# Retention of layer 0: keys placed by VectorE, one batch of look-ahead on TensorE, norm statistics at the end

## The chip, the cores and the metric

One core of a Trainium2 chip runs the whole program. The metric is the device time of one execution in microseconds (us); the kernel before takes 947.5 us in the median of three runs.

## The reference, cut to what matters

The input is 4 batches of 1024 tokens with 128 features, in fp32. After a layer norm, two branches run on it and their sum is added to the input: a retention block (16 heads of 8 features, with its own feed-forward block) and a two-layer local attention network (8 heads of 64, window 64, rotary positions, GELU feed-forward). The change touches the retention:

```python
q = l2_normalize(xn @ qw.T); k = l2_normalize(xn @ kw.T); v = xn @ vw.T
dmask = where(causal, gammas[:, None, None] ** (n - m), 0.0)
sim = einsum('bhnd,bhmd->bhnm', qh, kh) * scale * dmask
yh = einsum('bhnm,bhmd->bhnd', sim, vh)
y = yh.transpose(0, 2, 1, 3).reshape(B, T, D) @ ow.T + ob
```

The kernel computes it block-wise: inside blocks of 32 tokens by masked scores, between blocks and tiles by a carried sum of keys times values per head, with the decay folded into queries and keys.

## The kernel before, in words

Time is cut into 8 tiles of 128 tokens for each of 2 layers of the attention network, 16 steps in all. A step has four slots, one for each batch. `run_bodies` unrolls them, and each engine has its own order written out by hand; every dependency is a semaphore. In a slot, TensorE turns (transposes) the queries and keys of the batch two slots back, computes values for the new batch, scores, turned softmax weights, output turns, the query and key product into pQK, and the weighted values. VectorE takes maxima, subtracts, rotates (`dve_rotate`: cos, then sin, reading pQK), normalises outputs. GpSimd turns the sum of squares into a reciprocal norm (`pool_norm`, L450 and L452), adds the two rotated halves (`pool_add`, L465) and scales (`pool_scale`, L472). ScalarE evacuates PSUM and does exponentials.

In layer 0, the fourth slot of each step also starts the retention of the same tile, and a stretch behind it, called the retention here, finishes it: `pe_retention`, `dve_retention`, `act_retention`, `pool_retention`. For each batch b:

- `pe_retention_project` (L1573): q, k, v of the batch into a PSUM bank (pV or the upper half of pT).
- `act_retention_project` (L731, L736): sums of squares of q and k, then copies of v into avm.
- `pool_retention_norm` (L480, L482): reciprocal norms, ars.
- `dve_retention_qk` (L989): queries and keys times norm and decay, into aqk.
- TensorE turns both (L1587) into pM; ScalarE copies both to aqkT (L755, 128x256).
- `pool_mask_qk` places the keys (kx, L513, which lies in the tensor `hidden`) and the queries (qx, L517, in prT) so that heads of a group don't mix.
- `pe_block_values` (L1607) gives values turned; `act_place_values` (L746) places them in vx. `pe_block_sums` (L1618) gives keys times values per block, which VectorE masks into `before` (L1002).
- `pe_block_scores` (L1654) into pQK, once the rotation of batch 3 has been read out of it; `dve_block_scores` (L1013) applies the causal mask into sm.
- `pe_block_output` (L1628, L1634, L1641) adds the three parts of the output.

TensorE's loop runs k = 0 to 4: turn k, scores k-1, project k+2, placed values and sums k, output k-1. The statistics of the layer norm of the tile before (`pe_ln` L1394 and L1396, `dve_ln` L952 and L955, `pool_ln` L458 and L460) stand in iteration 3. In the next slot VectorE first applies that norm (`dve_ln_apply`, L962) and then adds the retention's residual (`dve_retention_out`, L1021), for which the scores of that slot (`pe_scores`, L1242 and L1255) wait. In the fourth slot VectorE's order is: L989 of retention batch 0, residual of the step before (L912), rotation cos (L842), softmax output (L900, L902), L989 of batch 1, rotation sin, sum of squares (L855). The retention's output is copied by ScalarE at L763 and multiplied at L1660.

Of the kernel before, what the change touches and what calls it, by code (L numbers as in the profile page):

```python
# [12 lines left out]
P = 128  # L13
# [80 lines left out]
def program(nc, a, out):  # L94
    with ExitStack() as ctx:
# [126 lines left out]

        def score_bank(b):

            return pQK[:, 512 * (b % 2):512 * (b % 2) + 512]
# [258 lines left out]
        def pool_retention(eng, t, old):  # L484
            last = NB - 1
            n = count((0, t), last)
            pool_retention_norm(eng, t, 1)
            for b in range(NB):
                pool_mask_qk(eng, t, b)
                if b + 2 < NB:  # L490
                    pool_retention_norm(eng, t, b + 2)
            if old:
                pool_ln(eng, old)
            pool_norm(eng, n, last)
            pool_add(eng, n, last)
            pool_scale(eng, n, last)
            pool_state(eng, t)
# [9 lines left out]
        def pool_mask_qk(eng, t, b):  # L507
# [86 lines left out]
        def act_slot(eng, new, old, ff, k):  # L594
# [30 lines left out]
            if k == NB - 1 and new and new[0] == 0:  # L625
                act_retention_project(eng, new[1], 0)
# [21 lines left out]
            if k == NB - 1 and new and new[0] == 0:  # L648
                act_retention_project(eng, new[1], 1)
# [74 lines left out]
        def act_retention_project(eng, t, b):  # L724
            n = 4 * t + b
            bank = qkv_banks[b % 2]
            eng.wait_ge(A["qkv_mm"], n + 1)
            need(eng, A["rs"], n - 1)
            for g in range(2):
                need(eng, A["sqq"], 2 * n + g)  # L730
                eng.activation(asq[:, :], bank[:, g * P:(g + 1) * P], ACT.Square,  # L731
                               accum_out=ass[:, b % 2, g:g + 1]).then_inc(A["sqq"], 1)
            need(eng, A["kv_mm"], n - 1)
            for c_ in range(NBL):
                rows = slice(0, (c_ + 1) * BL)
                copied = eng.activation(avm[rows, b % 2, c_, :], bank[rows, 2 * P:3 * P], ACT.Copy)  # L736
            copied.then_inc(A["v"], 1)

# [11 lines left out]
        def act_retention(eng, t, old):  # L750
            for k in range(NB):
                n = 4 * t + k
                eng.wait_ge(A["t_mm"], n + 1)
                need(eng, A["qx"], n - 1)
                eng.activation(aqkT[:, k % 2, :, :], pM[:, 0:256].rearrange("p (g n) -> p g n", g=2),  # L755
                               ACT.Copy).then_inc(A["t_ev"], 1)
                if k == 0:
                    act_exp(eng, 1, count((0, t), 1))
                act_place_values(eng, t, k)
                if k + 2 < NB:  # L760
                    act_retention_project(eng, t, k + 2)
# [71 lines left out]
        def dve_rotate(eng, step, k, weighted, ff=None, normed=None):  # L833
# [19 lines left out]
            def sum_squares():  # L853
                need(eng, S["max_ss"], n - 1)
                eng.tensor_reduce(ss[:, k % 2, :], sq[:, :].rearrange("p (h d) -> p h d", d=DH), AX.X,  # L855
                                  ALU.add).then_inc(S["ss_done"], 1)

            if k == NB - 1 and l == 0:
                dve_retention_qk(eng, t, 0)
                if normed:  # L860
                    dve_residual(eng, normed, k)
                eng.wait_ge(S["sq_done"], n + 1)
                turn_cos()
# [3 lines left out]
                turn_sin()  # L867
                sum_squares()
# [4 lines left out]
            sum_squares()  # L873
# [9 lines left out]
            turn_sin()  # L883

# [107 lines left out]

        def dve_retention(eng, t, old):
            eng.wait_ge(LS["qkn_done"], 4 * t + 3)
            for k in range(NB + 1):
                if k > 0:
                    dve_block_scores(eng, t, k - 1)
                if k < NB:
                    n = 4 * t + k
                    eng.wait_ge(A["kv_mm"], n + 1)  # L1000
                    need(eng, A["state"], t)
                    eng.tensor_tensor(before[:, k, :, :], pS[:, 0:P].rearrange("p (c n) -> p c n", c=NBL),  # L1002
                                      same_head, ALU.mult).then_inc(A["kvm"], 1)
                if k + 2 < NB:
                    dve_retention_qk(eng, t, k + 2)
                if k == NB - 1 and old:
                    dve_ln(eng, old)
# [295 lines left out]
        def pe_slot(eng, new, old, ff, k):  # L1303
# [271 lines left out]

        def pe_retention(eng, t, old):

            eng.wait_ge(LS["pt_ev"], 4 * t + 1)
            if old:
                eng.wait_ge(LS["xr_done"], count(old, NB - 1) + 1)  # L1580
            for k in range(NB + 1):
                if k < NB:
                    n = 4 * t + k
                    eng.wait_ge(A["qk"], 2 * n + 2)
                    need(eng, A["t_ev"], n)
                    for g in range(2):
                        mm = eng.transpose(pM[:, g * P:(g + 1) * P], aqk[:, k % 2, g, :], ident)  # L1587
                    mm.then_inc(A["t_mm"], 1)
                if k > 0:
                    pe_block_scores(eng, t, k - 1)  # L1590
                if k + 2 < NB:
                    pe_retention_project(eng, t, k + 2)
                if k == NB - 1 and old:
                    eng.wait_ge(A["t_ev"], 4 * t + 4)
                    pe_ln(eng, old)
                if k < NB:
                    pe_block_values(eng, t, k)
                    pe_block_sums(eng, t, k)
                if k > 0:
                    pe_block_output(eng, t, k - 1)  # L1600
# [142 lines left out]
```

## Time and profile before

| what | value |
|---|---|
| runs | 947.5, 945.47, 947.5 us; median 947.5 |
| profiled execution | 948.3 us, span of its trace 946.5 us |
| mean granted clock of TensorE | 0.989 of full |
| TensorE, matmuls | 863.4 us busy, 91% of the span |
| VectorE | 634.5 us, 67% |
| ScalarE | 559.2 us, 59% |
| GpSimd | 631.5 us, 67% |

Rows of a timeline give start, length, engine, line, operation, output and inputs, count, and in brackets the idle time before with what ended it. PE is TensorE's matmuls, PEld its weight loads, DVE VectorE, ACT ScalarE, POOL GpSimd. Matmuls are pipelined: the starts of the weight loads show how fast a group of them issues. A group's length on PE includes the latency of its last one. Tile 3 is the fourth of eight in layer 0; its retention output is copied at 274.77 us.

### The profile page before, as it was taken

The page shows a single profiled execution, that of the slowest core. Times are in us where ns is not written, and L with a number is a line of the kernel's source. Part 1 is how long each engine was busy: PE and PEld are TensorE (multiplying, and loading weights), DVE is VectorE, ACT ScalarE, POOL GpSimd, SP SyncE. Part 2 cuts the span into 40 slices and gives each one's busy share as a digit, 9 for nine tenths or more (in the row PEclk, how much of TensorE's full clock was granted, in tenths as well). Part 3 has the DMA queues.
Part 4 walks back from the last instruction along what each step waited for, and adds up shares of the span by engine and source line. Part 5 has one row for each costly group of instructions (what it writes and reads, how often), then busy time and mean ns, then how long its engine had stood idle before and what let it go on. Part 6 is the DMA issues. An engine that isn't in the chain of part 4 may idle for free.

```text
span 946.5 us, 26551 instructions
## 1 busy us (share of the span) xinstructions
PE 863.4 (91%) x10918; PEld 587.4 (62%) x10918; DVE 634.5 (67%) x1087; ACT 559.2 (59%) x1109; POOL 631.5 (67%) x503
## 2 busy tenths in 40 slices
PE   0678899989989899899998989999999999999998
PEld 0346666666666667666576565757575757575756
DVE  5875575766757666667576776767676767676754
ACT  0335575666756657567566555666666666666663
POOL 4588586676775876758667666676767676767641
PEclk9979999999999999999999999999999999999999
DMA  9211120211201112021021111212121212121201
GB/s 297 52 26 23 35 46 17 46 23 26 55 17 38 30 22 53 11 40 41 16 46 22 32 43 26 54 26 65 37 65 37 65 37 67 37 66 35 57 1 35
DMA packets 127890, 41.82 MB, mean 44 GB/s; under 512 B 103794, under 2 KB 127004, under 8 KB 127644
## 3 DMA queue, kind: packets, MB, share of 16 engines
q1 hardware_dynamic: 122516, 38.82, 18.3%
q10 hardware_dynamic: 5256, 1.31, 0.8%
q8 instruction: 88, 1.44, 0.6%
q14 instruction: 30, 0.25, 0.1%
HBM read 9.70 MB, written 2.10 MB: 12 GB/s over the span
## 4 chain that ended last, share of the span: by engine, by line
PE 62%; DVE 15%; POOL 10%; ACT 6%; issue 5%; DMA 1%; DVEq 0%; SPq 0%; POOLq 0%; ACTq 0%
PE pQK L1352 9%; PE pT L1266 5%; PE pT L1223 5%; PE pV L1321 5%; PE pS L1255 5%; PE pS L1282 4%; DVE m L842 4%; PE pM L1434 4%; PE pM L1300 4%; POOL rn L452 3%; PE pQK L1654 3%; PE pT L1412 3%; DVE ss L855 2%; POOL m L465 2%; PE pS L1242 2%
## 5 line engine op out<-in xcount | busy, mean ns | idle before, releaser
L452 POOL TENSOR_TENSOR rn<-rn,half_neg 128x16 f32<-128x16 f32 x64 | 187.5, 2929 | 5.3
L465 POOL TENSOR_TENSOR m<-m 128x1024 f32<-128x1024 f32 x64 | 150.7, 2355 | 0.0
L450 POOL TENSOR_SCALAR rn<-ss 128x16 f32<-128x16 f32 x64 | 16.3, 254 | 187.7 <-DVE ss L855 186.4
L1352 PE MATMUL pQK<-wqkv,hT 128*128 128x512 f32 x256 | 125.0, 611 | 5.2 <-DVE m L842 5.2
L472 POOL TENSOR_TENSOR qkn<-m,rn 128x1024 f32<-128x1024 f32 x64 | 121.7, 1902 | 5.0
L890 DVE TENSOR_REDUCE mx<-pS 128x8 f32<-128x1024 f32 x64 | 78.0, 1219 | 60.8 <-PE pS L1255 60.7
L672 ACT ACTIVATE prT<-pT 128x1024 f32<-128x1024 f32 x64 | 65.5, 1024 | 68.8 <-PE pT L1266 68.6
L635 ACT ACTIVATE sq<-pQK 128x1024 f32<-128x1024 f32 x64 | 65.4, 1022 | 35.4 <-PE pQK L1352 35.2
L855 DVE TENSOR_REDUCE ss<-sq 128x16 f32<-128x1024 f32 x64 | 77.6, 1212 | 7.1 <-ACT sq L635 6.9
L666 ACT ACTIVATE kT<-pT 128x512 f32<-128x512 f32 x64 | 38.2, 597 | 72.8 <-PE pT L1223 72.8
L892 DVE TENSOR_TENSOR pr<-pS,mx 128x1024 f32<-128x1024 f32 x64 | 78.4, 1225 | 2.2
L707 ACT ACTIVATE pr<-pr 128x1024 f32<-128x1024 f32 x64 | 67.3, 1051 | 18.8 <-DVE pr L892 18.6
L842 DVE TENSOR_TENSOR m<-pQK,rope 128x1024 f32<-128x1024 f32 x64 | 76.3, 1215 | 0.0
L842 DVE TENSOR_TENSOR m<-pQK,tab 128x1024 f32<-128x1024 f32 x64 | 76.2, 1212 | 0.0
L1282 PEld LDWEIGHTS pS<-vmix,prT 128*64 128x64 f32 x1024 | 64.5, 137 | 18.5 <-issue 13.1
L1223 PE MATMUL pT<-cst,qkn 128*128 128x128 f32 x512 | 70.4, 282 | 5.6 <-POOL qkn L472 4.9
L1321 PE MATMUL pV<-wqkv,hT 128*128 128x512 f32 x128 | 69.7, 628 | 5.7 <-DVE gst L1121 2.7
L1282 PE MATMUL pS<-vown,prT 128*64 128x65 f32 x1024 | 73.3, 225 | 0.0
L1282 PE MATMUL pS<-vmix,prT 128*64 128x65 f32 x1024 | 73.3, 225 | 0.0
L1352 PEld LDWEIGHTS pQK<-wqkv,hT 128*128 128x128 f32 x256 | 45.4, 195 | 42.8 <-issue 32.7
L1266 PE MATMUL pT<-cst,pr 128*128 128x128 f32 x512 | 70.0, 280 | 0.0
L1255 PE MATMUL pS<-kT,qT 64*64 64x128 f32 x2048 | 68.5, 273 | 0.0
(224 smaller groups left out, 1878.2 us busy)
## 6 DMA issues: line engine op xcount, KB each, us to landing
vmix<-vown SPq DMA_DIRECT2D x124, 128.0 KB, 2.7
kT<-kT SPq DMA_DIRECT2D x60, 128.0 KB, 2.6
x<-in_L_attn_x SPq DMA_DIRECT2D x4, 512.0 KB, 8.9
hT<-xnT SPq DMA_DIRECT2D x64, 32.0 KB, 1.9
xs<-in_L_attn_x SPq DMA_DIRECT2D x8, 256.0 KB, 3.1
hT<-x2T SPq DMA_DIRECT2D x64, 32.0 KB, 1.9
out<-aqkT SPq DMA_DIRECT2D x7, 256.0 KB, 2.2
wqkv<-in_L_ffn_wqkv SPq DMA_DIRECT2D x2, 768.0 KB, 9.6
```

Source lines behind the costliest of these rows:

```text
L452: eng.tensor_tensor(rn[:, k % 2, :], rn[:, k % 2, :], half_neg[:, 0:2 * H], ALU.pow).then_inc(S["rn_done"], 1)
L465: eng.tensor_tensor(m1[:, k % 2, :], m1[:, k % 2, :], m2[:, :], ALU.add).then_inc(S["add_done"], 1)
L472: eng.tensor_tensor(qkn[:, k % 2, :].rearrange("p (h d) -> p h d", d=DH), m1[:, k % 2, :].rearrange("p (h d) -> p h d", d=DH), rn[:, k % 2 ...
L842: eng.tensor_tensor(m.rearrange(shape, g=2, h=H, **sizes), src, by, ALU.mult).then_inc(S["mul_done"], 1)
L855: eng.tensor_reduce(ss[:, k % 2, :], sq[:, :].rearrange("p (h d) -> p h d", d=DH), AX.X, ALU.add).then_inc(S["ss_done"], 1)
L892: eng.tensor_tensor(pr[:, b % 2, :, :], sc, mx[:, :].unsqueeze(2).broadcast_to([P, H, P]), ALU.subtract).then_inc(S["sub_done"], 1)
L1223: mm = eng.transpose(pT[:, j * P:(j + 1) * P], qkn[:, b % 2, j * P:(j + 1) * P], ident)
L1255: mm = eng.matmul(pS[64 * w:64 * w + 64, col0:col0 + P], qT[r, j, 64 * w:64 * w + 64], keys, start=False, stop=True, skip_group_check=True)
L1266: mm = eng.transpose(pT[:, j * P:(j + 1) * P], pr[:, b % 2, j, :], ident)
L1282: mm = eng.matmul(pS[64 * w:64 * w + 64, col0:col0 + DH + 1], prT[:, i, 64 * w:64 * w + 64], (vown if w else vmix)[b][:, 2 * j + g, :], st ...
L1321: eng.matmul(pV[:, :], hT[:, k, :], wqkv[:, l, 1024:1536], start=True, stop=True).then_inc(S["v_mm"], 1)
L1352: mm = eng.matmul(pQK[:, g * 512:(g + 1) * 512], hT[:, k, :], wqkv[:, l, g * 512:(g + 1) * 512], start=True, stop=True)
```

## The change

- The keys are placed by VectorE (`dve_place_keys`) straight from the turned PSUM bank, with the same shape as before on GpSimd; ScalarE copies only the turned queries (128x128), and GpSimd places only queries. For batch 0, this placement waits for the weighted values of the slot, since qx shares its memory with the softmax weights.
- Turn 0 moves into the fourth slot, ahead of the weighted values, and writes to pT; turns 1 to 3 use pM.
- TensorE runs placed values and block sums of batch b+1 ahead of the output of batch b, and turns b+1 behind scores b.
- The layer-norm statistics move behind scores 3 on TensorE, and behind the last causal mask on VectorE.
- GpSimd scales batch 2 after the retention norm of batch 0. The orders on ScalarE and VectorE are written out; the sum of squares of batch 3 and the exponential of batch 1 stand near their ends.

```diff
+def turned_bank(b):
+    return pM if b else pT
...
     retain = k == NB - 1 and new and new[0] == 0
+    if k == 2 and new and new[0] == 0:
+        pool_norm(eng, count(new, k), k)
+        pool_add(eng, count(new, k), k)
+        return
     if retain:

         pool_retention_norm(eng, new[1], 0)
+        pool_scale(eng, count(new, 2), 2)
         return
     if old and k == NB - 1:
         pool_ln(eng, old)
...
     last = NB - 1
     n = count((0, t), last)
+    pool_place_queries(eng, t, 0)
     pool_retention_norm(eng, t, 1)
-    for b in range(NB):
-        pool_mask_qk(eng, t, b)
-        if b + 2 < NB:
-            pool_retention_norm(eng, t, b + 2)
+    pool_retention_norm(eng, t, 2)
+    pool_place_queries(eng, t, 1)
+    pool_retention_norm(eng, t, 3)
+    pool_place_queries(eng, t, 2)
+    pool_place_queries(eng, t, 3)
     if old:
...
+def pool_place_queries(eng, t, b):
     n = 4 * t + b
     shape = [P, NBL, NG, BL]
     eng.wait_ge(A["t_ev"], n + 1)
-    need(eng, A["st_mm"], n - 1)
-    eng.tensor_tensor(kx[:, b % 2, :, :, :],
-                      aqkT[:, b % 2, 1, :].rearrange("p (c n) -> p c n", c=NBL).unsqueeze(2).broadcast_to(shape),
-                      place_mask.unsqueeze(1).unsqueeze(3).broadcast_to(shape), ALU.mult).then_inc(A["kx"], 1)
+    if b == 0:
+        eng.wait_ge(LS["o_mm"], count((0, t), 0) + 1)
     need(eng, A["y_mm"], n - 1)
     eng.tensor_tensor(qx[:, b % 2, :, :, :],
                       aqkT[:, b % 2, 0, :].rearrange("p (c n) -> p c n", c=NBL).unsqueeze(2).broadcast_to(shape),
...
+
+def act_retention_queries(eng, t, b):
+    n = 4 * t + b
+    eng.wait_ge(A["t_mm"], n + 1)
+    need(eng, A["qx"], n - 1)
+    eng.activation(aqkT[:, b % 2, 0, :], turned_bank(b)[:, 0:P], ACT.Copy).then_inc(A["t_ev"], 1)
 def act_place_values(eng, t, b):
...
     placed.then_inc(A["vx"], 1)

 def act_retention(eng, t, old):
...
+    act_retention_queries(eng, t, 0)
+    act_retention_values(eng, t, 1)
+    act_retention_squares(eng, t, 2)
+    act_place_values(eng, t, 0)
+    act_retention_values(eng, t, 2)
+    act_retention_queries(eng, t, 1)
+    act_place_values(eng, t, 1)
+    act_retention_squares(eng, t, 3)
+    act_retention_queries(eng, t, 2)
+    act_retention_values(eng, t, 3)
+    act_place_values(eng, t, 2)
+    act_retention_queries(eng, t, 3)
+    act_exp(eng, 1, count((0, t), 1))
+    act_place_values(eng, t, 3)
     eng.wait_ge(A["y_mm"], 4 * t + 4)
     eng.activation(ayT, pY, ACT.Copy).then_inc(A["yt"], 1)

...
     if k == NB - 1 and l == 0:
         dve_retention_qk(eng, t, 0)
+        eng.wait_ge(S["sq_done"], n + 1)
+        turn_cos()
         if normed:
             dve_residual(eng, normed, k)
-        eng.wait_ge(S["sq_done"], n + 1)
-        turn_cos()
+        dve_place_keys(eng, t, 0)
+        turn_sin()
         if weighted:
             dve_output(eng, weighted[2])
         dve_retention_qk(eng, t, 1)
-        turn_sin()
-        sum_squares()
         return
...
+def dve_place_keys(eng, t, b):
+    n = 4 * t + b
+    shape = [P, NBL, NG, BL]
+    eng.wait_ge(A["t_ev"], n + 1)
+    need(eng, A["st_mm"], n - 1)
+    eng.tensor_tensor(kx[:, b % 2, :, :, :],
+                      turned_bank(b)[:, P:2 * P].rearrange("p (c n) -> p c n", c=NBL).unsqueeze(2).broadcast_to(shape),
+                      place_mask.unsqueeze(1).unsqueeze(3).broadcast_to(shape), ALU.mult).then_inc(A["kx"], 1)
+def dve_block_sums(eng, t, b):
+    eng.wait_ge(A["kv_mm"], 4 * t + b + 1)
+    need(eng, A["state"], t)
+    eng.tensor_tensor(before[:, b, :, :], pS[:, 0:P].rearrange("p (c n) -> p c n", c=NBL),
+                      same_head, ALU.mult).then_inc(A["kvm"], 1)
 def dve_retention(eng, t, old):
+    dve_block_sums(eng, t, 0)
     eng.wait_ge(LS["qkn_done"], 4 * t + 3)
...
+    dve_block_scores(eng, t, 0)
+    dve_place_keys(eng, t, 1)
+    dve_retention_qk(eng, t, 2)
+    dve_block_sums(eng, t, 1)
+    dve_block_scores(eng, t, 1)
+    dve_place_keys(eng, t, 2)
+    dve_retention_qk(eng, t, 3)
+    dve_block_sums(eng, t, 2)
+    dve_block_scores(eng, t, 2)
+    dve_place_keys(eng, t, 3)
+    dve_block_sums(eng, t, 3)
+    dve_sum_squares(eng, count((0, t), NB - 1), NB - 1)
+    dve_block_scores(eng, t, 3)
+    if old:
+        dve_ln(eng, old)
 def dve_block_scores(eng, t, b):
     n = 4 * t + b
...
+    if k == NB - 1 and new and new[0] == 0:
+        pe_retention_turn(eng, new[1], 0)
...
+def pe_retention_turn(eng, t, b):
+    n = 4 * t + b
+    eng.wait_ge(A["qk"], 2 * n + 2)
+    need(eng, A["kx"], n)
+    for g in range(2):
+        mm = eng.transpose(turned_bank(b)[:, g * P:(g + 1) * P], aqk[:, b % 2, g, :], ident)
+    mm.then_inc(A["t_mm"], 1)
 def pe_retention(eng, t, old):
...
     if old:
         eng.wait_ge(LS["xr_done"], count(old, NB - 1) + 1)
...
+    pe_retention_project(eng, t, 2)
+    eng.wait_ge(A["kx"], 4 * t + 1)
+    pe_block_values(eng, t, 0)
+    pe_block_scores(eng, t, 0)
+    pe_block_sums(eng, t, 0)
+    pe_retention_turn(eng, t, 1)
+    pe_block_values(eng, t, 1)
+    pe_retention_project(eng, t, 3)
+    pe_block_sums(eng, t, 1)
+    pe_block_output(eng, t, 0)
+    pe_block_scores(eng, t, 1)
+    pe_retention_turn(eng, t, 2)
+    pe_block_values(eng, t, 2)
+    pe_block_sums(eng, t, 2)
+    pe_block_output(eng, t, 1)
+    pe_block_scores(eng, t, 2)
+    pe_retention_turn(eng, t, 3)
+    pe_block_values(eng, t, 3)
+    pe_block_sums(eng, t, 3)
+    pe_block_output(eng, t, 2)
+    pe_block_scores(eng, t, 3)
+    if old:
+        eng.wait_ge(A["kx"], 4 * t + 4)
+        pe_ln(eng, old)
+    pe_block_output(eng, t, 3)
 def pe_block_values(eng, t, b):
```

## Rows read from the trace of the kernel before

**Rows 1.** The page: engine shares

```profile
PE 863.4 (91%) x10918; PEld 587.4 (62%) x10918; DVE 634.5 (67%) x1087; ACT 559.2 (59%) x1109; POOL 631.5 (67%) x503
```

**Rows 2.** Busy time by engine in one retention stretch

```profile
core 0: us, PE busy (x) PEld busy (x) DVE busy (x) ACT busy (x) POOL busy (x), PEclk, DMA share, GB/s
...
253.70:274.77 21.07, 17.85 (x514) 14.06 (x513) 11.78 (x32) 12.52 (x55) 15.48 (x21) 1.00 0.09 18
```

**Rows 3.** Timeline of tile 3, front edge of the retention

```profile
254.13 1.90 POOL L472 TENSOR_TENSOR qkn<-m,rn 128x1024 f32<-128x1024 f32 x1
...
254.13 0.19 ACT L731 ACTIVATION_READ_ACCUMULATOR asq<-pV 128x1 f32 x1
...
255.40 1.05 PE L1300 MATMUL pM<-oT,wo 128*128 128x128 f32 x8
...
257.05 0.61 DVE L989 SCALAR_TENSOR_TENSOR aqk<-pV,ars,cst 128x128 f32<-128x128 f32 x2 [3.19 <-POOL ars L482]
...
257.31 0.22 PE L1282 MATMUL pS<-vmix,prT 128*64 128x65 f32 x1
...
259.14 0.69 DVE L902 TENSOR_TENSOR o<-pS,rec 128x512 f32<-128x512 f32 x1
...
260.26 1.22 DVE L842 TENSOR_TENSOR m<-pQK,rope 128x1024 f32<-128x1024 f32 x1
...
261.39 1.21 DVE L855 TENSOR_REDUCE ss<-sq 128x16 f32<-128x1024 f32 x1
```

**Rows 4.** Timeline of tile 3: TensorE in the loop

```profile
262.53 0.81 PE L1573 MATMUL pT<-aT,xa 128*128 128x384 f32 x2
...
264.60 0.20 PEld L1587 LDWEIGHTS pM<-cst,aqk 128*128 128x128 f32 x2
...
268.57 0.20 PEld L1587 LDWEIGHTS pM<-cst,aqk 128*128 128x128 f32 x2
...
268.88 0.97 PEld L1654 LDWEIGHTS pQK<-prT,hidden 128*128 128x128 f32 x8
...
269.77 0.47 PEld L1394 LDWEIGHTS pM<-cst,xr 128*128 128x128 f32 x4
...
270.79 0.35 PEld L1607 LDWEIGHTS pT<-aT,xa 128*32 128x32 f32 x32
...
271.04 0.21 PEld L1618 LDWEIGHTS pS<-avm,aqk 128*32 128x32 f32 x8
...
271.18 0.28 PEld L1628 LDWEIGHTS pS<-prT,state 128*32 128x32 f32 x8
...
272.13 0.97 PEld L1654 LDWEIGHTS pQK<-prT,hidden 128*128 128x128 f32 x8
```

**Rows 5.** Timeline of tile 3: ScalarE, GpSimd and VectorE in the loop

```profile
266.50 1.10 ACT L746 ACTIVATE vx<-pT 32x128 f32<-32x128 f32 x4
...
267.77 1.04 POOL L517 TENSOR_TENSOR prT<-aqkT,cst 128x512 f32<-128x512 f32 x1
...
270.08 0.69 DVE L1013 TENSOR_TENSOR m<-pQK,cst 128x512 f32<-128x512 f32 x1 [1.84 <-PE pQK L1654]
```

**Rows 6.** Timeline of tile 3: the tail and the next slot

```profile
271.76 0.88 DVE L952 BATCH_NORM_STATS2 lbst<-pM 128x6 f32<-128x128 f32 x4
...
274.53 1.37 DVE L962 TENSOR_SCALAR hn<-pM,lmv,lrs 128x128 f32<-128x128 f32 x4 [0.51 <-POOL lrs L460]
...
274.77 0.60 ACT L763 ACTIVATE gg<-pS 128x512 f32<-128x512 f32 x1 [2.33 <-PE pS L1641]
...
276.64 0.75 DVE L1021 SCALAR_TENSOR_TENSOR x<-pS,col,xnT 128x512 f32<-128x512 f32 x1 [0.75 <-PE pS L1660]
...
286.81 0.26 POOL L450 TENSOR_SCALAR rn<-ss 128x16 f32<-128x16 f32 x1 [3.63 <-DVE ss L855]
```

**Rows 7.** Timeline of tile 0, front edge and retention output

```profile
76.21 0.61 DVE L989 SCALAR_TENSOR_TENSOR aqk<-pV,ars,cst 128x128 f32<-128x128 f32 x2 [1.33 <-POOL ars L482]
...
94.66 0.60 ACT L763 ACTIVATE gg<-pS 128x512 f32<-128x512 f32 x1 [3.33 <-PE pS L1641]
```

More of the change, by code:

```diff
@@ L505, in pool_state @@
             eng.tensor_tensor(state[:, :, :], state[:, :, :], before[:, :, NBL - 1, :], ALU.add).then_inc(A["state"], 1)
-        def pool_mask_qk(eng, t, b):
+        def pool_place_queries(eng, t, b):
             n = 4 * t + b
@@ L625, in act_slot @@
             if k == NB - 1 and new and new[0] == 0:
-                act_retention_project(eng, new[1], 0)
+                act_retention_squares(eng, new[1], 0)
+                act_retention_values(eng, new[1], 0)
             if k == 0 and turned:
@@ L648, in act_slot @@
             if k == NB - 1 and new and new[0] == 0:
-                act_retention_project(eng, new[1], 1)
+                act_retention_squares(eng, new[1], 1)
             else:
@@ L722, in act_gelu, with act_retention_squares @@
                            bias=b1e[0:m, l, 1, k:k + 1]).then_inc(S["gelu_done"], 1)
-        def act_retention_project(eng, t, b):
+        def act_retention_squares(eng, t, b):
             n = 4 * t + b
-            bank = qkv_banks[b % 2]
             eng.wait_ge(A["qkv_mm"], n + 1)
@@ L730, in act_retention_project, with act_retention_values @@
                 need(eng, A["sqq"], 2 * n + g)
-                eng.activation(asq[:, :], bank[:, g * P:(g + 1) * P], ACT.Square,
+                eng.activation(asq[:, :], qkv_banks[b % 2][:, g * P:(g + 1) * P], ACT.Square,
                                accum_out=ass[:, b % 2, g:g + 1]).then_inc(A["sqq"], 1)
-            need(eng, A["kv_mm"], n - 1)
+        def act_retention_values(eng, t, b):
+            need(eng, A["kv_mm"], 4 * t + b - 1)
             for c_ in range(NBL):
                 rows = slice(0, (c_ + 1) * BL)
-                copied = eng.activation(avm[rows, b % 2, c_, :], bank[rows, 2 * P:3 * P], ACT.Copy)
+                copied = eng.activation(avm[rows, b % 2, c_, :], qkv_banks[b % 2][rows, 2 * P:3 * P], ACT.Copy)
             copied.then_inc(A["v"], 1)
+        def act_retention_queries(eng, t, b):
[3 more added lines that the diff above has]
+            eng.activation(aqkT[:, b % 2, 0, :], turned_bank(b)[:, 0:P], ACT.Copy).then_inc(A["t_ev"], 1)
         def act_place_values(eng, t, b):
@@ L750, in act_retention @@
         def act_retention(eng, t, old):
[L751 to L761, printed above, removed]
+            act_retention_queries(eng, t, 0)
[12 more added lines that the diff above has]
+            act_place_values(eng, t, 3)
             eng.wait_ge(A["y_mm"], 4 * t + 4)
@@ L851, in turn_sin @@
                 turn(m2[:, :], rot, sin, "p (g h s d) -> p g h s d", s=2, d=32)
[L853 to L856, printed above, removed]
             if k == NB - 1 and l == 0:
                 dve_retention_qk(eng, t, 0)
+                eng.wait_ge(S["sq_done"], n + 1)
+                turn_cos()
                 if normed:
                     dve_residual(eng, normed, k)
-                eng.wait_ge(S["sq_done"], n + 1)
-                turn_cos()
+                dve_place_keys(eng, t, 0)
+                turn_sin()
                 if weighted:
@@ L872, in dve_rotate @@
             eng.wait_ge(S["sq_done"], n + 1)
-            sum_squares()
+            dve_sum_squares(eng, n, k)
             if weighted:
@@ L883, in dve_rotate, with dve_sum_squares @@
             turn_sin()
+        def dve_sum_squares(eng, n, k):
+            need(eng, LS["max_ss"], n - 1)
+            eng.tensor_reduce(ss[:, k % 2, :], sq[:, :].rearrange("p (h d) -> p h d", d=DH), AX.X,
+                              ALU.add).then_inc(LS["ss_done"], 1)
         def dve_scores(eng, b, n):
@@ L991, in dve_retention_qk @@
                                          op1=ALU.mult).then_inc(A["qk"], 1)
+        def dve_place_keys(eng, t, b):
[11 more added lines that the diff above has]
+                              same_head, ALU.mult).then_inc(A["kvm"], 1)
         def dve_retention(eng, t, old):
+            dve_block_sums(eng, t, 0)
             eng.wait_ge(LS["qkn_done"], 4 * t + 3)
[L995 to L1007, printed above, removed]
+            dve_block_scores(eng, t, 0)
[13 more added lines that the diff above has]
+                dve_ln(eng, old)
         def dve_block_scores(eng, t, b):
@@ L1574, in pe_retention_project @@
                        stop=True).then_inc(A["qkv_mm"], 1)
+        def pe_retention_turn(eng, t, b):
[5 more added lines that the diff above has]
+            mm.then_inc(A["t_mm"], 1)
         def pe_retention(eng, t, old):
-            eng.wait_ge(LS["pt_ev"], 4 * t + 1)
             if old:
                 eng.wait_ge(LS["xr_done"], count(old, NB - 1) + 1)
[L1581 to L1600, printed above, removed]
```

## The prediction

> **What bounds the kernel now.** I read the page's engine shares first: TensorE is busy 91% of the span [rows 1]. That is an average over stages, so I cut out the stage that the change touches, the retention of layer 0, eight times one tile, and asked for the busy time in one such stretch [rows 2]: in 21.07 us TensorE is busy 17.85, VectorE 11.78, ScalarE 12.52, GpSimd 15.48. No engine is full. Then I read the timeline of tile 3 in that stretch, front edge, middle and tail. All layouts below are for tile 3, in us from the span's start.
>
> Front edge: GpSimd starts the 1.90 us scale of batch 2 at 254.13, though the squares of retention batch 0 are ready at 254.13 + 0.19 = 254.32; VectorE's normalised queries and keys (L989) begin only at 257.05 after 3.19 idle [rows 3]. Middle: the weight loads of TensorE give the spacing of its groups when nothing holds them [rows 4]. One batch costs 0.31 (turn) + 0.89 (scores) + 0.25 (placed values) + 0.14 (block sums) + 0.95 (output) = 2.54 us, where before takes about 4 us (turn of batch 2 at 264.60, of batch 3 at 268.57). The causal mask L1013 of batch 2 follows 1.84 us of idle VectorE [rows 5]: the loop is turn, ScalarE copy, two GpSimd placements of 1.04 one behind the other, scores, mask, output. Tail: norm statistics L952 at 271.76, norm applied at 274.53, block residual x at 276.64, for which the next slot's scores wait; the retention output is copied at 274.77 [rows 6].
>
> **The change, part by part.**
>
> *GpSimd.* Four key placements (1.04 each, like the query placement [rows 5]) leave each tile. The scale of batch 2 goes behind the norm of retention batch 0. That norm took from about 256.0 to 257.0 (from the end of the scale to the start of L989), so 1.0. New: 254.4 to 255.4, scale to 257.3. Who needs the scale: the mask of batch 0 and the next slot's turn, both after 260.
>
> *VectorE.* L989 of batch 0: 255.5 to 256.1, 1.6 earlier. Rotation cos (1.22, and 1.13 from start to start [rows 3]) to 257.2, residual to 257.4. Added: key placement of batch 0. No row shows it; it reads PSUM, 128x512, with a broadcast. Below it the mask L1013 of the same shape, 0.69 [rows 5]; above it the 128x1024 rotation, 1.22 [rows 3]. Taken 0.69, same size and same source. 257.3 to 258.0. Rotation sin to 259.1 (before 260.26 + 1.22 = 261.5), output of batch 0 to 260.0 (before 259.14 + 0.69 = 259.8).
>
> *TensorE, front.* Output projection ends at 255.40 + 1.05 = 256.45 [rows 3]. New and ahead of the values: the turn of batch 0, issued 256.3 to 256.6, result 256.8. It waits for L989, done 256.1: no wait. Values, 0.93 (before, from about 256.4 to the last one at 257.31 [rows 3]), issued to 257.5, results at 257.85. Projection of batch 2, 0.84 with its issue gap (0.81 matmul [rows 4]), to 258.4; placed values 0 to 258.6. Scores 0 wait for rotation sin: 259.2 instead of 261.5. Sums 0 at 260.1.
>
> *New waits on GpSimd.* The placement of queries 0 now waits for the last value matmul, and the norm of batch 1 is queued behind it: 257.9 to 258.9, norm to 260.0. VectorE's L989 of batch 1 waits for it to 260.0 and ends at 260.65, 0.3 later than before. Turn 1 on TensorE 260.7. So TensorE idles here 0.55 + 0.5.
>
> *The loop.* Turn 1, placed values 1, projection 3, sums 1: 260.7 + 0.31 + 0.25 + 0.84 + 0.14 = 262.2. Output 0 to 263.2, scores 1 to 264.1, turn 2 to 264.4, placed values and sums to 264.8, output 1 to 265.7 (mask 1: scores end 264.35, 0.69, so 265.1, in time). Scores 2 need queries 2: turn result 264.55, ScalarE copy 0.25, GpSimd 1.04, so 266.0; to 266.9. Turn 3 to 267.2, values and sums 267.6, output 2 to 268.55; queries 3 give scores 3 at 268.8, to 269.7. (The 128x128 ScalarE copy: between 0.19 and the 0.60 of a 128x512 one [rows 3, 6]; taken 0.25, four times smaller data; at 0.6 it adds 0.35 in two places.) Period 3.1 to 3.3, against 4.
>
> *Hidden moves.* ScalarE is busy 12.52 of 21.07 [rows 2], 1.10 a batch for placed values [rows 5]; placed values 3 end near 269.8 and are used at 271.2. The exponential of batch 1 moves to about 267.7 to 268.7; its reader is a turn in the next slot, after 275. The sum of squares of batch 3 (1.21 [rows 3]) runs on VectorE at 268.6 to 269.8 while scores 3 are computed; mask 3 could not start before 270.0. GpSimd's norm of batch 3 stands behind the layer norm, both 0.9 earlier than before; GpSimd idles 3.63 before its next norm [rows 6], so this has cover. SP: the value copy that follows the values comes 0.35 later; its reader is a slot away.
>
> *Norm statistics.* Their transposes move from before placed values 3 to behind scores 3: 269.77 to 270.79 before, 1.02 [rows 4]; now 269.7 to 270.7, result 270.85. So the batch loop gains 3.3 us at scores 3 (272.13 before [rows 4]) and the norm's place gives all of it back to the norm. Statistics to norm applied is 274.53 - 271.76 = 2.77; now 270.9 + 2.77 = 273.65, 0.9 earlier. Norm applied 1.37, so the block residual can start at 275.0. By the other branch output 3 goes to 271.7, copied at 271.85 (2.9 earlier), and from the copy to the block residual is 276.64 - 274.77 = 1.87, so 273.7. VectorE's order puts the norm first: 275.0 decides, against 276.64. **Gain 1.6 per tile**; 1.3 of the 2.9 are lost to the new wait, which takes the place of 0.75 idle.
>
> Tile 0 has no norm of a tile before. Its squares are ready late anyway, L989 of batch 0 stands at 76.21 [rows 7]. By the same steps turn 1 falls at 81.2, and from turn 1 to the copy is 271.85 - 260.7 - 1.0 (no norm) = 10.2. Copy at about 91.5 to 92, against 94.66: gain 3.0.
>
> **Sum.** 948.3 (the profiled run, 946.5 span and 1.8 around it) - 7 x 1.6 - 3.0 = 934.1. The median of runs, 947.5, lies 0.8 below the profiled run; I leave that in the range. Forecast 934.
>
> *A rule against it.* TensorE's record is busy for 17.85 of 21.07 us [rows 2], and the change removes none of its work; GpSimd and ScalarE are less busy. The Trainium skill, Perfetto Trace Analysis, Identifying the Most-Contended Engine, has one optimise the engine with the highest occupancy, which here would promise nothing from moving vector work; the same section warns that matmul busy time misleads. The loads, busy 14.06 of 21.07 [rows 2], agree with the warning.
>
> *A second.* VectorE's rotation and sum start 1.13 apart though the first lasts 1.22 [rows 3]. The Trainium skill, VectorE: DVE Perf Modes, The DRAIN you can't avoid, says that an operation starts only when the pipe is empty, with exceptions; by full lengths the front would be some 0.4 longer and the sum 3 us higher. This trace shows the overlap, so the rows stand.
>
> **The rivals.**
> *Front edge not released.* If TensorE's new turn or GpSimd's new wait comes out later (key placement at 1.22, or the norm of batch 0 held up by work in between), up to 1.6 goes. With 1.22: 0.53 a batch, less the slack of 0.1 at L989, of 0.3 at scores 2 and 3, makes about 0.9 at the norm: gain 0.7 x 7 + 2 = 7, so 941. For it: TensorE, GpSimd and VectorE each wait on each other at 260. Against: nothing shown on VectorE with this shape costs over 0.69. Times 938 to 944.
> *Norm hidden.* If the layer norm didn't decide, 7 x 2.9 + 3 = 23, so 925. Against: the order on VectorE.
> *No change,* as the busy share of TensorE taken as its limit has it: each batch at the recorded lengths (about 3.5 us) leaves nothing: 948. Against: the spacings [rows 4].
> *Slower: the norm too late.* Everything from the norm's transposes to the next scores is a fixed 5.3 us after scores 3. It decides when these end after 269.7 + 1.6 = 271.3. Should the loop keep its 4 us, because VectorE now carries placement, mask, sums and L989 and is a step in both its halves, scores 3 end at 272.13 + 0.89 = 273.0: 1.7 per tile lost, 948.3 + 12 = 960. For it: keys, mask and sums in one queue, three waits per batch. Against: that is 0.69 + 0.69 + 0.61 [rows 3, 5] and the small mask of the sums, some 2.3 of 3.2.
>
> **How the numbers follow.** Norm decides, 0.52 (930 to 938). Front not released, 0.22. Norm hidden, 0.08. No change, 0.07. Slower, 0.11. A difference of 0.3%, 2.8 us, is about what a measurement of this kernel tells. Faster 0.82, same 0.07, slower 0.11. Range 925 to 943: from the norm hidden to the top of the second case; left out is 0.18.
>
> **What would show it.** VectorE's L989 near 255.5 relative to the same slot, key placement 0.69, turns 3 to 3.3 us apart; the retention output copied 2.9 earlier but the block residual only 1.6 earlier, VectorE going straight from the applied norm to it, and TensorE idle about 2 before the next slot's first scores; stretches after this unchanged in length. Wrong if the placement takes over 0.9, if turns stay 4 apart, or if GpSimd's norm of batch 1 comes after 261.

## The result, and the profile after

The changed kernel takes 936.48 us in the median of four runs (932.63 to 938.07), the kernel before 946.49 beside it (944.82 to 947.5): ratio 0.989, 95% interval 0.9855 to 0.9925, some 10 us faster. The prediction was 934 with a range of 925 to 943. Its profiled execution took 936.44, span 934.6, against 948.3 and 946.5.

The page of the changed kernel, engine shares and the shares of the chain that ended last:

```profile
PE 862.5 (92%) x10918; PEld 587.3 (63%) x10918; DVE 654.5 (70%) x1119; ACT 555.6 (59%) x1109; POOL 599.9 (64%) x471
...
PE 68%; DVE 14%; ACT 6%; issue 5%; POOL 4%; DMA 1%; DVEq 0%; SPq 0%; POOLq 0%; ACTq 0%
```

TensorE does the work of before (863.4 us) in a shorter span; 32 instructions moved from GpSimd to VectorE. The same stretch of tile 3 as [rows 2], from the same point to the copy of the retention output, busy time by engine (columns as there):

```profile
248.63:267.80 19.17, 18.04 (x514) 14.13 (x513) 14.15 (x35) 12.18 (x55) 10.05 (x14) 1.00 0.10 19
```

It lasts 19.17 instead of 21.07, and TensorE's busy time hardly moves (18.04 after 17.85): what went is its waiting. Against [rows 3] all times of tile 3 stand 5.07 earlier at the start of the stretch (the last read of a square sum at 249.06 against 254.13). Timeline of the front edge:

```profile
249.06 0.19 ACT L740 ACTIVATION_READ_ACCUMULATOR asq<-pV 128x1 f32 x1
...
249.64 0.71 POOL L491 TENSOR_TENSOR ars<-ars,half_neg 128x2 f32<-128x2 f32 x1
...
250.33 1.90 POOL L481 TENSOR_TENSOR qkn<-m,rn 128x1024 f32<-128x1024 f32 x1
...
250.39 0.61 DVE L1011 SCALAR_TENSOR_TENSOR aqk<-pV,ars,cst 128x128 f32<-128x128 f32 x2 [1.60 <-POOL ars L491]
...
252.28 0.68 DVE L1021 TENSOR_TENSOR hidden<-pT,cst 128x512 f32<-128x512 f32 x1
...
252.88 1.21 DVE L863 TENSOR_TENSOR m<-pQK,rope 128x1024 f32<-128x1024 f32 x1
...
254.89 0.61 DVE L1011 SCALAR_TENSOR_TENSOR aqk<-pT,ars,cst 128x128 f32<-128x128 f32 x2
```

Queries and keys of batch 0 wait 1.60 instead of 3.19 for their norm, as laid out; the new placement of keys is L1021, 0.68. Timeline of TensorE in the loop, weight loads and one matmul:

```profile
255.59 0.20 PEld L1626 LDWEIGHTS pM<-cst,aqk 128*128 128x128 f32 x2 [0.20 <-DVE aqk L1011]
...
259.14 0.25 PEld L1626 LDWEIGHTS pM<-cst,aqk 128*128 128x128 f32 x2
...
262.02 0.25 PEld L1626 LDWEIGHTS pM<-cst,aqk 128*128 128x128 f32 x2
...
263.44 0.22 PE L1664 MATMUL pT<-aT,xa 128*32 128x32 f32 x1 [0.55 <-issue]
...
265.41 0.47 PEld L1438 LDWEIGHTS pM<-cst,xr 128*128 128x128 f32 x4
```

The turns are 3.55 and 2.88 apart (laid out 3.4 and 2.8), where before has 3.97 for the second of these distances [rows 4]. In the middle of the placed values of batch 3, TensorE then stops for 0.55 with nothing to wait for that the profile shows. The tail, against [rows 6]:

```profile
266.55 0.89 DVE L974 BATCH_NORM_STATS2 lbst<-pM 128x6 f32<-128x128 f32 x4
...
267.80 0.60 ACT L784 ACTIVATE gg<-pS 128x512 f32<-128x512 f32 x1 [2.96 <-PE pS L1698]
...
270.62 0.74 DVE L1063 SCALAR_TENSOR_TENSOR x<-pS,col,xnT 128x512 f32<-128x512 f32 x1
...
271.50 0.41 PE L1284 MATMUL pS<-mask 64*64 64x512 bf16 x4 [1.02 <-DVE x L1063]
```

The residual row has no idle time ahead of it any more (0.75 before): VectorE comes straight from the applied norm, and TensorE waits 1.02 for the residual. From the copy to the residual it is 270.62 - 267.80 = 2.82, against 1.87 before. In the tiles whose copy no stop has delayed it is 3.1 to 3.2. This distance is the best single reading of the case, and the table below has it for every kernel.

### The profile page after: what moved, and what is told of

Same layout as the page of the kernel before. It is cut to its first block, busy times and chain, and to the rows that moved or that the text cites. A ratio compares the mean times of both kernels' runs of the same rounds, so it can differ in the third digit from the quotient of the medians.

```text
span 934.6 us, 26589 instructions
## 1 busy us (share of the span) xinstructions
PE 862.5 (92%) x10918; PEld 587.3 (63%) x10918; DVE 654.5 (70%) x1119; ACT 555.6 (59%) x1109; POOL 599.9 (64%) x471
## 4 chain that ended last, share of the span: by engine, by line
PE 68%; DVE 14%; ACT 6%; issue 5%; POOL 4%; DMA 1%; DVEq 0%; SPq 0%; POOLq 0%; ACTq 0%
PE pQK L1394 9%; PE pT L1308 6%; PE pS L1324 5%; PE pS L1297 5%; PE pT L1265 5%; PE pV L1363 5%; PE pM L1478 4%; PE pQK L1711 4%; DVE m L863 4%; PE pM L1342 4%; PE pT L1456 3%; PE pS L1284 2%; DVE hn L984 2%; PE pM L1336 2%; POOL lrs L469 2%
## 5 line engine op out<-in xcount | busy, mean ns | idle before, releaser
L622 ACT ACTIVATE vown<-pV 128x512 f32<-128x512 f32 x64 | 38.2, 597 | 52.7 <-DMA vmix<-vown 29.6
```

## How the stage is measured in the experiments

Differences of a few us between single executions are not all made in the retention. The block residual of tile 0 stood anywhere from 92.97 to 96.52 us in the profiles of this study, whatever the kernel, and the change of layers, between the last residual and the first output DMA, took 125.5 to 131.9 us. So beside the times I read, from each timeline, the mean of the six distances between block residuals from tile 1 to tile 7, the shortest of them (a tile without stalls), and the distance from copy to residual in that tile. Where two tiles share the shortest distance, the last column is that of tile 7. The stage numbers come from one profiled execution of each kernel, whose time can lie some us off the median (short_norm: 930.1 against 933.6).

| kernel | median us | ratio to before, interval | mean per tile | shortest | copy to residual |
|---|---|---|---|---|---|
| before | 946.5 | | 61.28 | 60.99 | 1.86 |
| x1_first_before | 948.0 | 1.0009 (0.9994 to 1.0025) | 61.30 | 60.99 | 1.86 |
| short_norm_before | 951.2 | 1.0052 (1.0032 to 1.0072) | 61.41 | 60.98 | 1.86 |
| scale_only | 940.5 | 0.9937 (0.9914 to 0.9959) | 60.48 | 60.13 | 1.86 |
| the change | 936.5 | 0.989 (0.9855 to 0.9925) | 59.95 | 59.60 | 3.1 |
| scale_back | 947.9 | 1.0005 (0.9991 to 1.0018) | 61.52 | 61.15 | 3.2 |
| keys_twice | 944.2 | 0.9977 (0.9965 to 0.999) | 60.76 | 60.70 | 3.2 |
| keys_on_pool | 958.9 | 1.0131 (1.0108 to 1.0154) | 62.78 | 62.77 | 3.2 |
| norm_early | 933.2 | 0.985 (0.9819 to 0.9881) | 59.37 | 58.79 | 1.86 |
| short_norm | 933.6 | 0.987 (0.985 to 0.989) | 58.92 | 58.49 | 2.1 |
| x1_first | 928.3 | 0.9806 (0.9785 to 0.9826) | 58.85 | 58.50 | 1.87 |
| x1_norm_early | 932.9 | 0.9851 (0.9819 to 0.9884) | 59.30 | 58.78 | 1.86 |

## Does the norm decide in the changed kernel?

Six kernels on one question. First, VectorE's order in the next slot turned round; the residual's four BATCH_NORM_STATS move into `dve_retention_stats`.

```diff
+if old and k == 0 and old[0] == 0:
+    dve_retention_out(eng, old[1])
 if ff and k == 0 and not is_scaled_early(ff):
     dve_ln_apply(eng, ff)
-if old and k == 0 and old[0] == 0:
-    dve_retention_out(eng, old[1])
...
 if turned:
     dve_scores(eng, turned[1], turned[2])
+if old and k == 0 and old[0] == 0:
+    dve_retention_stats(eng, old[1])
```

> The changed kernel with VectorE's order in the next slot turned round: the block residual first, then the layer norm applied, and the residual's statistics behind the score maxima. Theory N (in the changed kernel the norm decides when the block residual starts): by the changed kernel's trace the residual stands 3.1 to 3.2 us after the copy of the retention output in most tiles, and 1.87 after it in the kernel before where only the output decided; the waits go down by 0.5 to 1.35 per tile, 8.1 over tiles 1 to 7, so 936.5 - 8 = 928.5 us. Rival T (TensorE or the path through the retention output decides, the norm's wait is covered): no change, 935.5 to 937.5. Rival D (the norm applied becomes late for its own turn on TensorE, a new wait): 0 to 3 us gained.

Measured 928.31 (926.42 to 929.75), theory N's number. Its timeline in tile 3:

```profile
265.78 0.60 ACT L784 ACTIVATE gg<-pS 128x512 f32<-128x512 f32 x1 [2.36 <-PE pS L1702]
...
267.65 0.75 DVE L1065 SCALAR_TENSOR_TENSOR x<-pS,col,xnT 128x512 f32<-128x512 f32 x1 [1.65 <-PE pS L1721]
...
268.32 1.36 DVE L986 TENSOR_SCALAR hn<-pM,lmv,lrs 128x128 f32<-128x128 f32 x4
```

VectorE again waits for the output's product before the residual, 1.87 after the copy, and the norm is applied behind it. The norm is not on the path any more, and its own turn has cover. This version beats both kernels, in an interval that doesn't touch that of the change. Its gain of 8.2 us matches the sum of the waits that the trace of the change shows over tiles 1 to 7 (copy to residual, less 1.86 each: 8.15). Rival D, a new wait at the norm's own turn, did not come.

The same edit on the kernel before:

> The kernel before with VectorE's order in the next slot turned round as in x1_first. Theory N: there the residual waited for the output's product in every tile with the norm done 0.65 to 1.56 earlier, so nothing is gained: 946.5 within 1.5 us. Rival (the order is worth its 8 us whatever the rest): 938.5.

Measured 948.04, ratio 1.0009, per tile 61.30 against 61.28: nothing. The order is worth something only where the norm comes late, which the change brought about.

The norm made shorter instead, in both kernels. The edit is in `pool_ln`:

```diff
+if step[0] == 0:
+    eng.tensor_scalar(lrs[:, :], lmv[:, :, 1], EPS, None, ALU.add).then_inc(S["ln_rs"], 1)
+    return
 eng.tensor_scalar(lvar[:, :], lmv[:, :, 1], EPS, None, ALU.add).then_inc(S["ln_eps"], 1)
-eng.wait_ge(S["ln_eps"], ct + 1)
+eng.wait_ge(S["ln_eps"], ct + 1 - NT)
```

> The changed kernel with the reciprocal root of layer 0's layer norm left out on GpSimd (variance plus epsilon is used as the factor, which changes the result of the feed-forward of layer 0): 1.04 us and its wait fewer between statistics and norm applied, 1.1 per tile. Theory N: up to 1.1 in each of seven tiles, in the ones with less slack less, 7 us: 929.5. Rival T: no change, 936.5.

> The same root left out of the kernel before. Theory N says that there the norm did not decide, since VectorE idled 0.65 to 1.56 before the block residual: no change, 946.5 within 1.5. A rival under which the root is on the path in both kernels: 939.5.

Both kernels leave the root out, so only their times are of use. By these both miss: 933.57 instead of 929.5, and 951.23 instead of 946.5. By the stage both hit. Per tile the changed kernel gains 59.95 - 58.92 = 1.03, and the distance from copy to residual falls from 3.1 to 2.1; the kernel before has 61.41 against 61.28 and 1.86 as ever. What hides it stands elsewhere: from the last block residual to the first output DMA short_norm_before takes 131.93 us where before takes 127.17, and short_norm 129.23 against the change's 127.01. The timeline of short_norm_before there shows two operations on 4 values each:

```profile
573.79 2.27 DVE L1134 TENSOR_TENSOR gtmp<-gst,gsc 128x4 f32<-128x4 f32 x1
576.10 1.99 DVE L1135 TENSOR_SCALAR gsh<-gtmp,col 128x4 f32<-128x4 f32 x1
```

In the kernel before the same two take 0.16 and 0.23, so 3.9 of the 4.8 us are these two. In short_norm they take 2.27 and 1.99 as well, but its change of layers is only 2.2 longer; the other 1.9 of its miss stay open. The last section shows what the two operations wait for.

Last, the norm moved forward in the retention, in the changed kernel and in x1_first.

```diff
+if old:
+    eng.wait_ge(A["kx"], 4 * t + 4)
+    pe_ln(eng, old)
 pe_block_scores(eng, t, 3)
-if old:
-    eng.wait_ge(A["kx"], 4 * t + 4)
-    pe_ln(eng, old)
...
 dve_block_sums(eng, t, 3)
-dve_sum_squares(eng, count((0, t), NB - 1), NB - 1)
-dve_block_scores(eng, t, 3)
 if old:
     dve_ln(eng, old)
+dve_block_scores(eng, t, 3)
+dve_sum_squares(eng, count((0, t), NB - 1), NB - 1)
```

> The changed kernel with the norm's transposes ahead of the scores of batch 3 on TensorE and its statistics ahead of the last causal mask on VectorE (the sum of squares goes last). The norm comes about 1 us earlier, the retention output about 0.7 later than in the changed kernel. Theory N: the block residual 0.6 earlier in seven tiles, 4 us, so 932.5. Rival T (the retention output decides): 0.7 later in seven tiles, 941.5.

> x1_first and norm_early together. With the block residual ahead of the applied norm, theory N says that the path through the retention output decides, and norm_early puts the norm's transposes and statistics on that path: the copy of the output came about 0.7 us later in an undisturbed tile there, so 0.5 to 0.7 later in seven tiles than x1_first, 928.3 + 4 = 932.5, the opposite sign of what norm_early did to the changed kernel alone (936.5 to 933.2). Rival (an early norm is good in itself, for GpSimd or for the next slot): at or below 928.

Measured 933.17 and 932.94: the same move gains 0.58 per tile on the changed kernel (59.95 to 59.37) and loses 0.45 on x1_first (58.85 to 59.30). In the shortest distances, where stops of TensorE play no part, it gains 0.81 and loses 0.28, and from L989 to the copy norm_early is 0.45 longer in tile 7 (17.03 against 16.58), not the 0.7 that was expected. By the intervals alone neither difference is certain, since each pair just overlaps; the signs in the stage and both medians are as theory N has them. In norm_early the residual is back to waiting for the output (copy, norm applied, residual of its tile 3):

```profile
268.86 0.60 ACT L784 ACTIVATE gg<-pS 128x512 f32<-128x512 f32 x1 [3.42 <-PE pS L1698]
268.93 1.36 DVE L984 TENSOR_SCALAR hn<-pM,lmv,lrs 128x128 f32<-128x128 f32 x4
...
270.72 0.75 DVE L1063 SCALAR_TENSOR_TENSOR x<-pS,col,xnT 128x512 f32<-128x512 f32 x1 [0.43 <-PE pS L1717]
```

Rival T fell in x1_first, short_norm and norm_early. In x1_first and x1_norm_early the path through the retention output is the one that decides, as theory N has it once the norm is out of the way.

## What holds the front edge and the loop?

The order of GpSimd alone, put into the kernel before (scale_only); scale_back takes the same lines out of the changed kernel:

```diff
+if k == 2 and new and new[0] == 0:
+    pool_norm(eng, count(new, k), k)
+    pool_add(eng, count(new, k), k)
+    return
 if retain:
     pool_retention_norm(eng, new[1], 0)
+    pool_scale(eng, count(new, 2), 2)
     return
```

> The kernel before with one edit: GpSimd does the scale of batch 2 behind the retention norm of batch 0. Theory F (the front edge is held by that scale, whatever the rest): VectorE's queries and keys of batch 0 come 1.6 us earlier, the rotation sin about 1.1 earlier, since the residual now waits for the output projection, so the scores of batch 0 come 1.0 earlier and, as the loop stays as it is, the block residual too: 1.0 in seven tiles, 7 us, so 939.5. Rival L (the gain comes from the look-ahead and the keys on VectorE): within 1 us of 946.5.

> The changed kernel with the scale of batch 2 put back in its slot, ahead of the retention norm. Theory F: VectorE's queries and keys of batch 0 come 1.6 later, and with them the turn of batch 0, the weighted values behind it, the output of batch 0 and the keys of batch 1: 1.5 later in seven tiles, 10.5 us, so 947, no faster than before. Rival L: the loop makes up for it, at most 3 us slower than the changed kernel, 939.5.

Measured 940.49 and 947.94, so rival L fell in both. One instruction's place brings 6 of the 10 us by itself, and without it the rest of the change brings nothing (ratio 1.0005). The first row of scale_back shows VectorE's wait as long as in [rows 3], 3.20, the second TensorE's wait for the turn of batch 0:

```profile
256.64 0.61 DVE L1011 SCALAR_TENSOR_TENSOR aqk<-pV,ars,cst 128x128 f32<-128x128 f32 x2 [3.20 <-POOL ars L491]
...
257.31 0.44 PE L1626 MATMUL pT<-cst,aqk 128*128 128x128 f32 x2 [1.27 <-DVE aqk L1011]
```

It costs more there (1.55 in the shortest tile) than it gives on the kernel before (0.86). The change put the turn of batch 0 ahead of the weighted values, and TensorE stands still for 1.27 in front of it: whatever makes queries and keys of batch 0 late now also holds these, the output of the slot and the keys behind them.

The keys back on GpSimd: the four calls of `dve_place_keys` go, and

```diff
 def pool_place_queries(eng, t, b):
...
+    need(eng, A["st_mm"], n - 1)
+    eng.tensor_tensor(kx[:, b % 2, :, :, :],
+                      aqkT[:, b % 2, 1, :].rearrange("p (c n) -> p c n", c=NBL).unsqueeze(2).broadcast_to(shape),
+                      place_mask.unsqueeze(1).unsqueeze(3).broadcast_to(shape), ALU.mult).then_inc(A["kx"], 1)
     if b == 0:
         eng.wait_ge(LS["o_mm"], count((0, t), 0) + 1)
...
-    eng.activation(aqkT[:, b % 2, 0, :], turned_bank(b)[:, 0:P], ACT.Copy).then_inc(A["t_ev"], 1)
+    eng.activation(aqkT[:, b % 2, :, :], turned_bank(b)[:, 0:2 * P].rearrange("p (g n) -> p g n", g=2),
+                   ACT.Copy).then_inc(A["t_ev"], 1)
```

And the keys placed twice on VectorE, in `dve_place_keys`:

```diff
+    spare = hn[:, :, :].rearrange("p c (g n) -> p c g n", g=NG)
+    for place in (spare, kx[:, b % 2, :, :, :]):
+        placed = eng.tensor_tensor(place,
...
+    placed.then_inc(A["kx"], 1)
```

> The changed kernel with the keys placed by GpSimd, ahead of the queries of the same batch, and ScalarE copying both, as before. If two placements of 1.04 in a row belong to the loop (theory P): 0.3 to 0.4 later at the front and 1.1 at scores 2 and at scores 3, 2.6 to 2.8 per tile in eight tiles, 22 us, so 955 to 959, slower than the kernel before. Rival O (the order alone brings the gain, TensorE being the limit in the loop): 936 to 940.

> The changed kernel with each placement of keys on VectorE done twice, once into a spare tile: 0.60 more per batch. By the layout of the prediction: 0.55 later at queries and keys of batch 1, 0.3 more at scores 2 and at scores 3, so 1.15 per tile in eight tiles, 9 us: 945.7. If VectorE is the bound of the loop (rival V), all four count in full: 2.4 per tile, 19 us: 955.5. If it has cover everywhere: 936.5.

keys_on_pool measured 958.86, slower than the kernel before by 1.3%, 3.2 per tile more than the change in the shortest tile (2.6 to 2.8 expected). Two placements stand one behind the other again, and the look-ahead has no slack for them. TensorE stands still for 1.30 before the scores; the profile names no releaser, but the queries that they need are placed until 263.96 + 1.04 = 265.00, and the scores before that start at 265.10:

```profile
262.96 1.04 POOL L524 TENSOR_TENSOR hidden<-aqkT,cst 128x512 f32<-128x512 f32 x1 [0.92 <-ACT aqkT L759]
...
263.96 1.04 POOL L530 TENSOR_TENSOR prT<-aqkT,cst 128x512 f32<-128x512 f32 x1
...
266.27 0.69 DVE L1056 TENSOR_TENSOR m<-pQK,cst 128x512 f32<-128x512 f32 x1 [2.13 <-PE pQK L1712]
...
269.09 1.13 PE L1712 MATMUL pQK<-prT,hidden 128*128 128x128 f32 x8 [1.30 <-issue]
```

The turns are 4.21 and 3.98 apart, as in the kernel before (4.20 and 3.98), while the norm comes at the end of the loop. So the look-ahead needs the keys spread over two engines; whether these bring anything in the old order of TensorE was not tried. keys_twice measured 944.24; the shortest tile is 60.70 against 59.60, 1.1 for 2.4 us of added VectorE work, where the layout had 1.15. Four operations of 0.60 are less than half on the path: the price of an operation there is read from slacks. Rival V, VectorE as the bound of the loop, fell (955.5), and with it the reason given for the slower case of the prediction.

## Why the prediction was right, and where it was off

**Front edge.** Right to 0.1. From L989 of batch 0, laid out at 255.5, to turn 1, at 260.7, it was 5.2; in the trace 255.59 - 250.39 = 5.20, the same in tiles 1 to 7 within 0.01. GpSimd's new wait and TensorE's new turn cost what was laid out.

**Key placement.** Taken 0.69 between 0.69 and 1.22: it is 0.68. The case *front edge not released* had no ground there. That nothing of this size on VectorE costs over 0.69 was misread: the block residual, 128x512, takes 0.75 [rows 6]. It did no harm. The case is priced up to 944, while the range that was to reach its top ends at 943.

**The loop.** Laid out from L989 to the norm's transposes: 269.7 - 255.5 = 14.2. In tile 7, which has no stall, it is 505.37 - 490.86 = 14.51, and from L989 to the residual 19.71 where 19.5 was laid out:

```profile
490.86 0.61 DVE L1011 SCALAR_TENSOR_TENSOR aqk<-pV,ars,cst 128x128 f32<-128x128 f32 x2 [1.60 <-POOL ars L491]
...
505.37 0.47 PEld L1438 LDWEIGHTS pM<-cst,xr 128*128 128x128 f32 x4
...
507.43 0.60 ACT L784 ACTIVATE gg<-pS 128x512 f32<-128x512 f32 x1 [2.21 <-PE pS L1698]
...
509.29 1.36 DVE L984 TENSOR_SCALAR hn<-pM,lmv,lrs 128x128 f32<-128x128 f32 x4 [1.48 <-POOL lrs L469]
510.57 0.74 DVE L1063 SCALAR_TENSOR_TENSOR x<-pS,col,xnT 128x512 f32<-128x512 f32 x1
```

The distance of residuals there is 59.60 against 60.99: a gain of 1.39 for the *gain 1.6 per tile*. The output's copy came 2.67 earlier (1.61 at L989, and 16.58 instead of 17.64 from there), where 2.9 was laid out. The rest is about 0.1 at each hand-over of the loop that the layout rounded away: the turns are 3.56 and 2.88 apart and the norm's transposes 2.87 behind the last, for 3.4, 2.8 and 2.8.

**The norm decides.** Right, and shown: the norm gave back 1.28 in tile 7 (3.14 against 1.86 from copy to residual) and 1.3 to 1.4 in tiles 1, 2, 4 and 5, where the prediction had 1.3. In tiles 3 and 6 the copy itself came late by a stop and the norm cost only 0.94 and 0.5. The prediction's TensorE idle of about 2 before the next slot's first scores is 1.02 in tile 3 and at most 1.39. The rivals *norm hidden*, *no change* and *slower* did not come. How near the slower one was can be seen in keys_on_pool: the loop keeps its 4 us, the norm comes behind it, and the time is 958.9, where the rival had 960, though it is GpSimd and not VectorE that holds the loop there.

**Tile 0: the term that was mis-sized.** *Gain 3.0* set a layout without any stop against a measured time that has stops in it. Measured from L989 of batch 0 to the copy, before takes 94.66 - 76.21 = 18.45 [rows 7], after 91.80 - 74.28 = 17.52:

```profile
74.28 0.61 DVE L1011 SCALAR_TENSOR_TENSOR aqk<-pV,ars,cst 128x128 f32<-128x128 f32 x2 [1.33 <-POOL ars L491]
...
89.06 0.26 PE L1698 MATMUL pS<-m,vx 128*32 128x32 f32 x4 [0.97 <-issue]
...
91.80 0.60 ACT L784 ACTIVATE gg<-pS 128x512 f32<-128x512 f32 x1 [2.77 <-PE pS L1698]
```

That is 0.9. Turn 1 came when laid out (5.06 behind L989; 5.0 laid out, though the same steps as in tile 3 give 5.2). From there to the copy it took 12.5 instead of 10.2: TensorE stopped for 0.56 and 0.97 with no wait shown, and the other 0.7 is rounding as in tile 7 and smaller gaps. The kernel before stops in its tile 0 too, for 0.52 and 0.84, and the 94.66 contains that. These two stops in the kernel before:

```profile
88.16 0.33 PE L1641 MATMUL pS<-m,vx 128*32 128x32 f32 x16 [0.52 <-issue]
...
91.92 0.26 PE L1641 MATMUL pS<-m,vx 128*32 128x32 f32 x4 [0.84 <-issue]
```

**The stops in other tiles.** L989 to residual is 19.71 in tiles 6 and 7 and 19.73 in tile 2, but 21.01, 20.23, 20.34 and 20.64 in tiles 1, 3, 4 and 5: 3.4 us in all. Tiles 1, 3 and 5 have stops of 0.34 to 0.73; what delays tile 4 the trace doesn't show, no gap there being over 0.23 before the one of 1.39 for the residual. The kernel before loses 2.5 us in the same way, above all in tiles 1, 5 and 6 (two of its distances are 61.75 and 61.90 where 60.99 is usual). So the mean gain of the six distances is 1.33, not 1.39. Tile 6 of the changed kernel has a stop of 0.61 too; it delays the copy by 0.8 against tile 7 and the residual not at all, which shows again that the norm decides there.

**Sum.** In the profiled pair the six distances bring 8.0 together, the distance from tile 0 to tile 1 brings 58.06 - 57.24 = 0.8, and tile 0 itself 0.9: 9.8 us, against 14.2 forecast and 10.0 by the medians. So 2.1 of the 4.4 that are missing belong to tile 0 and 2.3 to the seven tiles of *gain 1.6*. The whole profiled pair shows 11.9, of which 1.9 lie before the retention of tile 0 (L989 at 74.28 against 76.21), in a part that the change leaves alone and that scatters in every kernel here.

**The two rules.** TensorE's stretch went from 21.07 to 19.17 with its busy time unchanged, so here the bound engine's occupancy was raised by moving work on the others. By the loops, turns 2.88 apart are closer than the 3.5 us of recorded lengths that the rival *no change* took as a batch's floor. That agrees with the caution in the Trainium skill (Perfetto Trace Analysis, Identifying the Most-Contended Engine) that matmul busy time is no measure of the distance to the limit; where that limit lies no run here shows. The key placement starts at 252.28 and lasts 0.68, and the next rotation starts at 252.88, 0.60 later. What the Trainium skill says of an operation that starts only when the pipe is empty (VectorE: DVE Perf Modes, The DRAIN you can't avoid), taken without its exceptions, is not borne out by these two rows.

## What to carry to other kernels

When a step is moved out of a loop to its end, ask what it meets there: the norm's later place gave back half of what front edge and loop gained (1.3 of 2.7 us per tile), and putting the residual, for which TensorE waits, ahead of the norm, for which nobody does yet, took it back (928.3 us). Look for the single instruction in front of an engine's queue that delays a short one that others wait for; here it was worth 6 us alone and decided whether the larger rewrite paid at all. And cost an added operation by the slack at its place: four of 0.60 cost 1.1.

## What the runs showed of the hardware that was not expected

**Small operations of VectorE beside GpSimd.** The two operations on 4 values per partition that short_norm_before made longer, with GpSimd's rows beside them:

```profile
573.70 2.34 POOL L468 TENSOR_TENSOR m<-m 128x1024 f32<-128x1024 f32 x1
...
573.79 2.27 DVE L1134 TENSOR_TENSOR gtmp<-gst,gsc 128x4 f32<-128x4 f32 x1
576.10 1.99 DVE L1135 TENSOR_SCALAR gsh<-gtmp,col 128x4 f32<-128x4 f32 x1
576.12 1.90 POOL L475 TENSOR_TENSOR qkn<-m,rn 128x1024 f32<-128x1024 f32 x1
```

The first ends at 576.06, 0.02 after GpSimd's addition of the rotated halves; the second at 578.09, 0.07 after its scale. In the kernel before the first of the two runs beside another operation of GpSimd, the reciprocal root, and is short; GpSimd's addition starts only behind it, at 574.91:

```profile
572.01 2.93 POOL L452 TENSOR_TENSOR rn<-rn,half_neg 128x16 f32<-128x16 f32 x1
...
574.29 0.16 DVE L1131 TENSOR_TENSOR gtmp<-gst,gsc 128x4 f32<-128x4 f32 x1
```

It is so in all twelve traces: VectorE has 29 operations on 4 values that last over 0.4 us, and each ends 0.02 to 0.07 us after an addition or a scale of GpSimd ends. Two of them are in the kernel before (1.02 and 2.27). So the root left out moved GpSimd's work onto these operations. What the two engines share there, no run shows.

**Stops of TensorE.** The stops of 0.4 to 1.2 us for which the profile names no wait fall, with three exceptions, in the middle of runs of small matmuls where the program has no semaphore. They stay with the order of the program: in tile 0 a stop stands behind the 26th recorded matmul of one such run in the change and all its variants but keys_on_pool, and behind the 28th in the kernel before and its three variants. The page has a DMA queue for instructions, here that of the changed kernel (packets, MB, share of the engines' span):

```profile
q8 instruction: 88, 1.44, 0.7%
```

The trace keeps the time of each of its packets of 16384 bytes. Leaving out keys_on_pool, where regular waits before the scores carry the same label, the eleven other kernels have 51 such stops of over 0.4 us in the eight tiles, and every one of them ends 2.2 to 2.9 us after the start of such a packet, though the times that lie so make up only 15% of the retentions. Most packets bring no stop. That ties the stops to the loading of instructions in time; no experiment was made on it, so the cause is not shown.

Both are why two kernels should be compared by a stage and not by one span, when a few us matter.
